# Seventy-one routed blocks with one region per expert, and the last results gathered through two queues and summed with GpSimd's help

## The reference

```python
logits = xf @ gate_w + gate_b                 # xf: layer norm of the tokens
probs = softmax(logits)
top2_vals, top2_idx = top_k(probs, 2)         # two experts for each token
...
h = gelu(xf @ w1 + bb1)                       # 128 -> 256, for each expert
y = h @ w2 + bb2                              # 256 -> 128
acc = acc + we[:, None] * y                   # weighted by the gate's value
```

## Time and profile before

| what | value |
|---|---|
| time, median of 3 runs | 366.29 us (366.03 to 366.57) |
| time of the profiled execution | 366.62 us |
| span of the profiled execution | 364.8 us |
| PE busy | 308.3 us (85%) |
| DVE busy | 255.0 us (70%) |
| ACT busy | 224.9 us (62%) |
| POOL busy | 218.2 us (60%) |
| blocks, and sends on POOL | 78 |

### The profile page before, as it was taken

How to read it: one execution, slowest core, us unless ns; L and a number is a source line. 1 busy time by engine, 2 the same in 40 slices (tenths; PEclk the granted TensorE clock), 3 DMA queues, 4 the chain that set the end, 5 groups by cost and what they waited for, 6 DMA issues and landing times.

```text
span 364.8 us, 10711 instructions
## 1 busy us (share of the span) xinstructions
PE 308.3 (85%) x2560; PEld 267.9 (73%) x2560; DVE 255.0 (70%) x1083; ACT 224.9 (62%) x648; POOL 218.2 (60%) x320
## 2 busy tenths in 40 slices
PE   0899839999999999999999999986979989999500
PEld 0346439889898888989888888875969979998400
DVE  2984334788888888888888889776547646555583
ACT  1146345676767677676767766585577767766642
POOL 5000322347767767677776776367767777777760
PEclk9999957999999999999999999999899999999955
DMA  7947812223222222222222224442246343333973
GB/s 191 282 151 277 348 39 85 80 75 85 105 85 99 95 91 93 91 100 91 95 92 92 91 100 83 97 112 71 81 87 135 102 113 103 106 87 85 328 290 130
DMA packets 36059, 45.06 MB, mean 124 GB/s; under 512 B 7068, under 2 KB 27298, under 8 KB 35888
## 3 DMA queue, kind: packets, MB, share of 16 engines
q1 hardware_dynamic: 28896, 34.89, 31.1%
q0 software_dynamic: 4544, 8.44, 6.9%
q10 hardware_dynamic: 2576, 1.25, 1.2%
HBM read 30.57 MB, written 14.90 MB: 125 GB/s over the span
## 4 chain that ended last, share of the span: by engine, by line
PE 69%; issue 9%; ACT 7%; POOL 4%; DMA 4%; DVE 4%; ACTq 2%; SPq 1%; POOLq 0%; DVEq 0%
PE bank L1456 19%; PE bank L1446 18%; PE bank L1518 8%; PE bank L1510 7%; PE bank L1361 6%; ACT samp L780 5%; POOL result L626 4%; PE bank L1395 3%; DMA result<-y,rows_in 2%; PE bank L1373 2%; PE bank L1502 2%; PE bank L1349 1%; DMA rows_in<-routed 1%; PE bank L1470 1%; ACTq L704 1%
## 5 line engine op out<-in xcount | busy, mean ns | idle before, releaser
L626 POOL DMA_INDIRECT result<-y,rows_in x78 | 77.7, 997 | 25.9 <-issue 18.6
L1456 PE MATMUL bank<-filt_sb,samp 128*128 128x128 f32 x576 | 77.1, 283 | 4.3 <-ACT samp L780 3.7
L1446 PE MATMUL bank<-S,xwin 100*128 100x144 f32 x512 | 80.1, 307 | 0.0
L618 POOL DMA_INDIRECT routed<-payload,slot x64 | 63.9, 998 | 23.4 <-issue 15.6
L1456 PEld LDWEIGHTS bank<-filt_sb,samp 128*128 128x128 f32 x576 | 70.1, 194 | 9.2 <-ACT samp L780 7.8
L1446 PEld LDWEIGHTS bank<-S,xwin 100*128 100x128 f32 x512 | 69.5, 194 | 8.1 <-issue 7.2
L805 ACT ACTIVATE hid<-bank,w_blk 128x128 f32<-128x128 f32 x156 | 48.7, 364 | 30.4 <-PE bank L1510 29.0
L751 ACT ACTIVATE ysp<-bank 100x512 f32<-100x512 f32 (+1 forms) x96 | 46.6, 487 | 29.6 <-PE bank L1395 27.5
L780 ACT ACTIVATE samp<-bank 128x432 f32<-128x432 f32 (+1 forms) x96 | 47.1, 490 | 20.8 <-PE bank L1446 19.7
L970 DVE TENSOR_TENSOR S<-ysp,bank 100x512 f32<-100x512 f32 (+1 forms) x96 | 52.9, 552 | 9.8 <-ACT ysp L751 6.1
L1518 PE MATMUL bank<-w_all,hid 128*128 x312 | 52.9, 293 | 3.5 <-ACT hid L805 3.2
(11 more groups left out here) (119 smaller groups left out, 447.0 us busy)
## 6 DMA issues: line engine op xcount, KB each, us to landing
xwin<-lines SPq DMA_DIRECT2D x64, 120.0 KB
xwin<-lines SPq DMA_DIRECT2D x32, 160.0 KB
rows_in<-routed SPq DMA_DIRECT2D x78, 64.5 KB, 2.0
w_all<-in_experts SPq DMA_DIRECT2D x4, 642.0 KB, 10.9
x<-in_x_tiles SPq DMA_DIRECT2D x1, 2048.0 KB, 11.5
wide<-result SPq DMA_DIRECT2D x4, 512.0 KB, 5.2
wide<-in_x_rows SPq DMA_DIRECT2D x3, 512.0 KB, 8.8
lines<-wide SPq DMA_DIRECT2D x3, 512.0 KB, 7.0
```

The source lines that it names most:

```text
L618: nc.gpsimd.indirect_dma_start(routed, bass.IndirectOffsetOnAxis(slot[:, par, c2:c2 + 1], 0), payload[:, q, c2, :], None).then_inc((s.scat ...
L626: nc.gpsimd.indirect_dma_start(result, bass.IndirectOffsetOnAxis(rows_in[:, slot, C:C + 1].bitcast(U32), 0), y[:, slot, :], None, bounds_c ...
L1446: last = nc.tensor.matmul(bank[5 + (par + g) % 2][:, i * TAPS * TT:(i + 1) * TAPS * TT], xwin[:, q, t, :], weights[:, t], start=True, stop ...
L1456: last = nc.tensor.matmul(bank[7][:, 0:C], samp[:, par, j, :], filt_sb[:, order[j], :], start=(j == 0), stop=(j == TAPS - 1))
```

## The change

It has four parts.

1. **One region per expert.** The rows of an expert stand one behind another over all 32 bands; the subregions, the second set of ranks (`seen2`) and the first round of paddings are gone. The first part of the blocks takes only full blocks from the first SPLIT = 24 bands, of which there are at least 2 * 24 - 7 = 41. Everything else, including full blocks of the first 24 bands beyond the 41st and the incomplete ones, belongs to the second part of 30 blocks. The sum is 71 = (2 * 128 * 32 + 8 * 127) // 128. The paddings are written once, after the last count, and SP waits for them ahead of block 41.
2. **The plans.** The first has 11 links (steps of bands 26 and 27). A chain of 7 links (`carry`, one link in each of blocks 5 to 11) and the second plan of 16 links (two in each of blocks 12 to 19) follow; before, the second plan had 12 links in blocks 8 to 13. PE turns the second plan in block 22, DVE copies it in block 24. A plan's expert numbers are packed into words of eight blocks: the first plan now has 6 words and no longer 8; the second has 4 and no longer 3, and they are read on PE in block 36.
3. **The split.** With SPLIT = 24 there are six first groups of 4 bands, and SP loads them when block 54 has been sent (OLD_BLOCKS = 55). Four groups of 2 bands are left for the tail. The band loop makes 5 passes and no longer 6, and eight steps are straight code behind it.
4. **The tail.** Of the four last groups ACT loads the first and the third, SP the second and the fourth. The second group (POOL_GROUP, bands 26 and 27) is scaled by ACT alone, on both sides, and summed by POOL with two additions. SP stores the groups in order, so the stores of the third and fourth group stand behind the wait for POOL's sum. The scaled halves of the last groups go to PSUM banks of their own.

```diff
-SPLIT = 26
-PART_BANDS = (SPLIT, BANDS - SPLIT)
...
-PART_BLOCKS = tuple((2 * P * n + EXPERTS * (BLOCK - 1)) // BLOCK for n in PART_BANDS)
-FIRST_BLOCKS = PART_BLOCKS[0]
-BLOCKS = sum(PART_BLOCKS)
+SPLIT = 24
...
+FIRST_BLOCKS = 2 * SPLIT - (EXPERTS - 1)
+OLD_BLOCKS = most_blocks(SPLIT)
+BLOCKS = most_blocks(BANDS)
+PART_BLOCKS = (FIRST_BLOCKS, BLOCKS - FIRST_BLOCKS)
...
+POOL_GROUP = len(FIRST_BACKS) + 1
...
-            write_paddings(0)
-            sp.wait_ge(s.idle_written, 16)
             sp.wait_ge(s.plan_ready, 1)
...
                 if i == 26:
-                    write_paddings(1)
+                    write_paddings()
             sp.wait_ge(s.plan_ready, 2)
             part_written(1)
+            sp.wait_ge(s.idle_written, 16)
+            sp.wait_ge(s.pads_written, 16 * EXPERTS)
...
-            all_sent(sp, FIRST_BLOCKS)
+            all_sent(sp, OLD_BLOCKS)
             for g in range(len(FIRST_BACKS)):
                 load_back(g)
             for g, (b, n) in enumerate(BACKS):
                 if g == len(FIRST_BACKS):
                     all_sent(sp, BLOCKS)
-                sp.wait_ge(s.out_ready, g + 1)
+                    for h in range(g + 1, len(BACKS), 2):
+                        load_back(h)
+                if g == POOL_GROUP:
+                    sp.wait_ge(s.pool_out, 1)
+                else:
+                    sp.wait_ge(s.out_ready, g + (g < POOL_GROUP))
                 sp.dma_start(out[:, b:b + n, :], kept_rows(g)).then_inc(s.stored, 16)
...
+            both_rows, kept = y_back(POOL_GROUP), kept_rows(POOL_GROUP).rearrange("p b c -> p (b c)")
+            pool.wait_ge(s.scaled_both, 2 * BACKS[POOL_GROUP][1])
+            nc.gpsimd.tensor_tensor(both_rows[:, 0, :], both_rows[:, 0, :], both_rows[:, 1, :], ALU.add
+                                    ).then_inc(s.pool_sum, 1)
+            pool.wait_ge(s.pool_sum, 1)
+            nc.gpsimd.tensor_tensor(kept, kept, both_rows[:, 0, :], ALU.add).then_inc(s.pool_out, 1)
...
-                    for h in range(g, len(BACKS)):
+                    for h in range(g, len(BACKS), 2):
                         act.dma_start(y_back(h), result_rows(h)).then_inc(back_arrived[h], 16)
                 act.wait_ge(back_arrived[g], 16)
-                at_least(act, s.out_ready, g - 1)
+                if g == POOL_GROUP:
+                    for c2 in range(2):
+                        for j in range(n):
+                            rows = y_back(g)[:, c2, j * C:(j + 1) * C]
+                            nc.scalar.activation(rows, rows, ACT.Copy, scale=share[:, c2, b + j:b + j + 1]
+                                                 ).then_inc(s.scaled_both, 1)
+                    continue
+                if g < len(FIRST_BACKS):
+                    at_least(act, s.out_ready, g - 1)
...
-                if 8 <= i < 8 + PLAN_LINKS // 2:
-                    plan(1, 2 * (i - 8))
-                    plan(1, 2 * (i - 8) + 1)
+                if 5 <= i < 5 + CARRY_LINKS:
+                    carry(i - 5)
+                if 12 <= i < 12 + PLAN_LINKS // 2:
+                    last_plan(2 * (i - 12))
+                    last_plan(2 * (i - 12) + 1)
...
-                if i == 20:
-                    plan(1, PLAN_LINKS)
-                    plan(1, PLAN_LINKS + 1)
+                if i == 24:
+                    turned(1)
...
             for g in range(len(BACKS)):
-                combine(g)
+                if g != POOL_GROUP:
+                    combine(g)
...
-                if i == 17:
+                if i == 22:
                     turn_plan(1, BANDS)
-                if i == 40:
+                if i == FIRST_BLOCKS - 5:
                     experts_of += load_words(pe, mybir.EngineType.PE, 1, 0, SECOND_WORDS)
```

More of the change, by code:

```diff
@@ L102 @@
 N_EARLY = 4
-N_CLEARED = 11
+N_CLEARED = 12
 SLOW_LINKS = 55
@@ L1063, in run, with copy_count, thresholds, counts @@
                     chain(b, par, link)
-            def plan(part, link):
+            def copy_count(part):
+                dve.wait_ge(s.count_psum, part + 1)
+                nc.vector.tensor_copy(count[:, part, :], bank[7][:, AT_COUNT:AT_COUNT + EXPERTS]).then_inc(s.plan_step, 1)
+            def thresholds(first, n):
+                return table_sb[:, T_THRESH + first:T_THRESH + first + n].unsqueeze(1).broadcast_to([P, EXPERTS, n])
+            def counts(part, n):
+                return count[:, part, :].unsqueeze(2).broadcast_to([P, EXPERTS, n])
@@ L1077, in plan, with last_plan @@
+            def last_plan(link):
+                if link == 0:
+                    dve.wait_ge(s.plan_step, CARRIED)
+                    copy_count(1)
+                    return
+                dve.wait_ge(s.plan_step, CARRIED + link)
                 if link == 1:
-                    nc.vector.tensor_tensor(pad_row[:, part, :], count[0:1, :], table_sb[0:1, region:region + EXPERTS],
+                    nc.vector.tensor_tensor(pad_row[:, :], count[0:1, 1, :], table_sb[0:1, T_REGION:T_REGION + EXPERTS],
@@ L1092, in plan @@
                 elif link == 5:
-                    nc.vector.tensor_reduce(upto[:, :], tri_t[:, :, :], AX_X, ALU.add).then_inc(s.plan_step, 1)
+                    nc.vector.tensor_tensor(nblk[:, :], ends[:, 1:2 * EXPERTS + 1], starts[:, 0:2 * EXPERTS], ALU.subtract
+                                            ).then_inc(s.plan_step, 1)
                 elif link == 6:
-                    nc.vector.tensor_scalar(step_to[:, :], nblk[:, :], -float(BLOCK), float(REGION), ALU.mult, ALU.add
+                    for kind in range(2):
+                        last = nc.vector.tensor_tensor(
+                            tri_t[:, kind, :, :],
+                            nblk[:, kind * EXPERTS:(kind + 1) * EXPERTS].unsqueeze(1).broadcast_to([P, EXPERTS, EXPERTS]),
+                            tri, ALU.mult)
@@ L1256, in step @@
                     if known and b == SPLIT + 3:
-                        for link in range(6, PLAN_LINKS):
-                            plan(0, link)
+                        for link in range(6, FIRST_LINKS):
+                            first_plan(link)
                     residual(b - 1, other, 0)
@@ L1544, in _ @@
                 pe.wait_ge(s.win_1, 16 * WINDOW_LOADS)
-                for part, first, end in ((0, 0, SPLIT // 2), (1, SPLIT // 2, BANDS // 2)):
-                    with pe.Fori(first, end) as i:
-                        gathered_band(i * 2, 0, part)
-                        gathered_band(i * 2 + 1, 1, part)
-                count_part(0, BANDS)
+                with pe.Fori(0, SPLIT // 2) as i:
+                    gathered_band(i * 2, 0)
+                    gathered_band(i * 2 + 1, 1)
+                count_part(0, SPLIT)
+                pe.wait_ge(s.plan_step, 1)
+                with pe.Fori(SPLIT // 2, BANDS // 2) as i:
+                    gathered_band(i * 2, 0)
+                    gathered_band(i * 2 + 1, 1)
                 turn_plan(0, BANDS)
```

250 lines of the change are left out of this document (156 added, 94 removed).

## The result

The changed kernel takes 361.98 us (median of 4 runs, 360.44 to 362.32) against 366.43 us (366.03 to 367.07) for the kernel before: a ratio of 0.9869, with a 95% interval from 0.9837 to 0.9901. That is faster by 4.5 us, where 8.2 us were forecast. Two of the six executions of one kernel (e9_exp_late) took over 1.5% longer than its fastest and are left out of its time. The profiled execution took 362.17 us and has a span of 360.3 us, so 4.45 us less in time and 4.5 us less in span than the profiled execution of before.

A forecast was written before the change was run, and what follows sets the result against it. The prediction took POOL's unbroken queue of sends as the bound. Its terms, -9.1 - 0.5 - 0.1 + 0 + 0 + 1.5 = -8.2 us, took 366.29 to 358.1 us, with eight in ten from 356.4 to 360.0 us.

The forecast's parts named there:

- What bounds the kernel: Blocks' stage: POOL sends without pause, 0.98 us plus 0.30 us of its own each, while PE runs ahead.
- seven blocks fewer: POOL's queue: seven sends fewer at 1.299 us each save 9.1 us, 7.6 at the small end.
- Fewer words: PE's pause ahead of 256.00 us: reading 6 words, not 8, saves 0.5 us, between 0.3 and 0.75.
- the first plan: Band steps 26 and 27: plan two bands earlier and one link shorter, 0.1 us less, from -0.3 to +0.6.
- The longer second plan: DVE's links in blocks 5 to 19: 23 where it had 12, taken as 0, up to +1.5 us.
- that rival: Blocks 5 to 19: the second plan delays `finish` and the gap ahead of send 13 grows; 360.3 us, chance 0.12.
- The hand-over at block 41: SP reads the new plan's words and waits for paddings at block 41, not 59; taken as 0.
- the rival that has POOL run dry here: Block 41: loads issued too late for POOL, needing some 6.5 us; time above 367 us, chance 0.02.
- The tail: Behind the last send: two bands more to add up cost +1.5 us, from +0.4 to +2.3.
- Both signs of being wrong: POOL's sends idle beyond 0.30 us after block 20, or the tail's first landing over a microsecond later.
- The landing of the first data: Tail: 1 MB in two queues sharing the DMA engines moves the first landing by +0.4 us, 0 to 0.9.
- The chain and the stores: Tail: scalings, additions and SP's store issues put the last store 0.8 to 1.3 us later; taken as 1.1.

The follow-up runs named there:

- e9_exp_late: Changed kernel with VectorE summing all, last loads from ACT alone, PE's second words in block 41, exponentials in block 55, shares in block 60: 358.60 us, ratio 0.9778.
- e4_idle7: Changed kernel with seven more blocks holding only padding rows at the end, 78 again: 371.64 us, ratio 1.0151 to the kernel before.
- e1_dve_all: Changed kernel with POOL's sum in the tail given back to VectorE, loads still in two queues: 359.58 us, ratio 0.9834 to the kernel before.
- e10_split26: e9_exp_late with SPLIT back at 26, so three groups in the tail and still 71 blocks: 356.98 us, ratio 0.9753 to the kernel before.

## Why the forecast was wrong, step by step

**What bounds the kernel, and seven blocks fewer: right.** POOL's unbroken queue set the time. The term was 9.1 us, and seven of the old sends are 9.13; the kernel with seven blocks of padding more bears that out with 9.0 (e4_idle7). That sends took 0.018 us less each behind the change of tables was not forecast; it gave 1.0 us more.

**Fewer words, the first plan: right, with the words at the small end of their bounds in most profiles.** The stretch up to the send behind the change of tables became 0.51 us shorter (0.5 forecast) in the first profile, and 0.30 to 0.45 in the other six of kernels with that change in block 12. The gap ahead of that send was to be 1.3 us beyond the usual and was 1.4 in two of the seven and 1.7 in five; it was 1.82 before. In the chain of waits the step in which PE's sequencer reads words is 2.52 us and was 2.98. Steps 26 and 27 of the bands took 6.85 and 6.29 us, 6.57 in the mean, where 6.5 were expected, and the first send is 0.33 us earlier (0.1 forecast). Since the first send lies anywhere from 244.3 to 247.4 us in the profiles of this study, those 0.33 us prove nothing either way.

**The longer second plan: right.** Nothing between the send behind the change of tables and block 36 shows a lost microsecond, so that rival falls. The most that any profile has there is 0.5 us beyond the usual (e4_idle7, ahead of the send at 271.83 us).

**The hand-over at block 41: a term of nothing that measured 1.3 us in one profile and nothing in the other.** The forecast looked for the danger in SP's loads and in paddings. It didn't count that PE and VectorE read the words in the same block, one behind the other, nor PE's clock behind the pause. In the first profile the shorter sends gave back nearly as much, so it is luck that the sum up to the last send fits to 0.1 us. In the rival that has POOL run dry here, 2 us of loading and three periods of 1.09 us are 5.3 us and not 6.5; that only makes the rival weaker.

**The tail: the step that failed.** It was put at +1.5 us, with +2.3 as its upper end, and measured +5.14. Both signs of being wrong that the forecast named came true, idle time of POOL behind block 20 and a first landing over a microsecond later, but neither points at the largest part, which no term stood for. The parts:

- *The closing of POOL's queue* was not in the sum: +2.9 us. POOL's work in the tail was costed as two additions and SP's wait for them, and these came out as forecast ("POOL is done 3.5 us after the first landing"; measured 354.20 - 350.74 = 3.46). The step that failed is that POOL was taken to be done with its last addition, so that the end of its queue stood in the sum with nothing. That this end has a price of its own could have been read in the trace of before, where POOL's drain ended 6.45 us past its last send and only 3.5 us ahead of SP's. This is shown: the price goes when POOL's late work goes (e1_dve_all), comes into the kernel before with a wait alone, and vanishes there when the wait is early.
- *The landing of the first data* was put at +0.4 us with 0.9 as the bound and measured +1.39. The direction was right, the size was not. The rule cited from the Trainium skill (page "DMA: Bandwidth & Descriptors", section "Issuing engines are not separate DMA queues") holds as far as these runs go: two queues brought the first data no earlier, but some 0.5 to 1.0 us later than four loads in one queue. The rest, some 0.3 to 0.8 us, may have come with the fourth load itself (3.21 to 3.47 us against 2.67 to 2.93 in the four profiles of the kernel before and its variants). A kernel with three loads in one queue had 3.65 us, though (e10_split26), so the cause of this part is open.
- *The chain and the stores* were put at +1.1 us and measured 1.18 + 0.09.
- *The issue of the loads* came 0.42 us sooner behind the last send, which was not forecast.

With the drain taken out and VectorE summing all (e1_dve_all) the kernel is 6.05 us faster than the kernel before on the same chip, where 8.2 were forecast and 6.3 were the least that the range allowed. Its interval (4.5 to 7.7 us by the ratio) holds values on both sides of that. So the drain is the larger part of the miss, and not all of it.

**The spread.** The forecast took 0.73 us as what can be told from no change, from three runs within 0.54 us. The four larger groups of runs of the kernel before, of 7 to 17 runs, spread over 1.7 to 4.6 us; that is why several small gains above are not shown in time.

## What to carry to other kernels

Before an engine is given work near the end, look at when its queue closes: list the drains, see which one ends last, and how far the others lie ahead. A helper engine with a long closing must be out of work early: here SP's drain came 6.46 us after the first data of the tail, and POOL's closing alone takes 5.9 us from its last work in a kernel of 71 sends. That leaves less than 0.6 us, and one addition takes 0.72, so no sum of POOL's in the tail could have been free. When a bound is as plain as a queue of equal sends, take the saving from its period, and spend the care on what lies behind the last of them.

## What the runs showed of the hardware

- GpSimd's drain ended 5.9 to 6.5 us after its last work or its last wait, in all fourteen profiles, with work or without (the drain lasts 6.45 us behind a wait alone). It was 5.86 to 5.93 us with 71 sends and 6.44 to 6.52 with 78. Its record can begin long before the last work is done, as the 17.9 us of the kernel before show. VectorE's drain was 0.43 to 0.46 us, PE's 0.51 to 0.61 us.
- Four loads of 256 KB, issued two and two from SP and ACT, brought the first data 3.96 to 4.22 us after ACT's first issue; issued from ACT alone, 3.21 to 3.47 us.
- Behind a pause of 1.9 to 2.4 us PE's granted clock fell in six of ten profiles (means over 5 us of 0.66 to 0.76; in windows of 1 us it reads 0.50, the level of 1.2 GHz, in each of the six) and stayed at 1.00 in four, and the same kernel showed both.
- Sends with a median of 0.97 us, and not 0.98, appear only in the four profiles of kernels in which POOL adds tensors in the tail, and they do so long before these additions run. Why is open.
